# A fused state-space and MLP layer on one core: the squared halves added on VectorE before PE sums them, the x bias written by ScalarE, and four reorderings of the steady turn

## The reference

```python
x = L0_attn_x                                  # (8, 512, 128)
xn = _layernorm(x, axis=-1)
x = x + _L0_attn_ref(xn, ...) + _L0_ffn_ref(xn, ...)
```

```python
zxbcdt = x @ in_proj_w.T                       # z (256), xBC (256 + 128), dt (4)
dt = softplus(zxbcdt[..., -NHEADS:] + dt_bias)
conv = conv_b
for k in range(D_CONV):                        # 4 taps
    conv = conv + xp[:, k:k + L, :] * conv_w[:, k]
xBC = silu(conv)                               # x_ssm, B, C
theta = clip(theta_base + tanh(x @ theta_w1) @ theta_w2, ...)
log_z = complex(-lambda_eff * dt, theta * dt)  # decays and turns the state
# scan over chunks: y = Re(C . sum of exp(cumulated log_z) * B * (x_ssm * dt))
g = (y + x_ssm * D) * silu(z)
g = g * rsqrt(mean(g * g, axis=-1) + RMS_EPS) * norm_w      # 256 channels
return g @ out_proj_w.T
```

## Time and profile before

| | |
|---|---|
| time, median of 3 runs (lowest to highest) | 336.48 us (335.78 to 337.73) |
| the profiled execution: time, span of its instructions | 337.05 us, 334.9 us |
| granted TensorE clock, mean over the span | 0.964 of full |
| PE busy | 292.5 us, 87% |
| PE's weight loads | 210.1 us, 63% |
| DVE busy | 257.8 us, 77% |
| POOL busy | 190.9 us, 57% |
| ACT busy | 182.1 us, 54% |

### The profile page before, as it was taken

How to read it: one execution, slowest core, us unless ns; L and a number is a source line. 1 busy time by engine, 2 the same in 40 slices (tenths; PEclk the granted TensorE clock), 3 DMA queues, 4 the chain that set the end, 5 groups by cost and what they waited for, 6 DMA issues and landing times.

```text
span 334.9 us, 9439 instructions
## 1 busy us (share of the span) xinstructions
PE 292.5 (87%) x3927; PEld 210.1 (63%) x3927; DVE 257.8 (77%) x632; ACT 182.1 (54%) x336; POOL 190.9 (57%) x165
## 2 busy tenths in 40 slices
PE   1396679799999999999999999999899999968780
PEld 1253246587588758776678657875777577735680
DVE  4585788889788887988698878987798868887221
ACT  0587646287438844785567654774288445750110
POOL 1004253529990999279944997099918991684001
PEclk9879799999999999999999999999999999998795
DMA  7302300141012200230123001311022002301001
GB/s 204 82 0 50 78 0 2 33 97 33 31 35 68 61 18 25 77 78 2 33 57 91 16 31 41 76 45 33 3 64 66 3 31 50 81 0 34 2 2 37
DMA packets 19306, 14.85 MB, mean 44 GB/s; under 512 B 5077, under 2 KB 15034, under 8 KB 19258
## 3 DMA queue, kind: packets, MB, share of 16 engines
q1 hardware_dynamic: 17192, 13.83, 16.0%
q10 hardware_dynamic: 2066, 0.36, 0.6%
HBM read 3.70 MB, written 2.10 MB: 17 GB/s over the span
## 4 chain that ended last, share of the span: by engine, by line
PE 65%; DVE 10%; POOL 7%; ACT 6%; issue 3%; DMA 3%; SPq 2%; ACTq 1%; POOLq 0%; DVEq 0%
PE bank L1483 10%; PE bank L1534 7%; PE bank L1535 6%; PE bank L1585 4%; PE bank L1646 4%; PE bank L1545 4%; PE bank L1592 4%; PE bank L1555 4%; PE bank L1621 3%; PE bank L1636 3%; PE bank L1565 3%; ACT z L1107 2%; PE bank L1601 2%; PE bank L1523 2%; SPq L439 2%
## 5 line engine op out<-in xcount | busy, mean ns | idle before, releaser
L1332 POOL TENSOR_TENSOR btmp<-cims,X 128x512 f32<-128x512 f32 x15 | 19.1, 1272 | 68.0 <-DMA cims<-bc 53.0
L1534 PE MATMUL bank<-h0h,W 128*128 128x512 f16 x128 | 50.3, 393 | 6.9 <-DVE h1l L808 5.5
L1535 PE MATMUL bank<-h0l,W 128*128 128x512 f16 x128 | 50.0, 391 | 0.0
L1483 PE MATMUL bank<-XW,xh 128*128 128x256 f16 x256 | 48.3, 277 | 0.0
L1483 PE MATMUL bank<-XW,xl 128*128 128x256 f16 x128 | 35.3, 276 | 0.0
L1157 ACT ACTIVATE h1h<-bank 128x512 f16<-128x512 f32 x32 | 18.9, 593 | 22.7 <-PE bank L1535 22.7
L808 DVE SCALAR_TENSOR_TENSOR h1l<-bank,h1h 128x512 f16<-128x512 f32 x32 | 21.9, 687 | 11.0 <-ACT h1h L1157 10.9
L1483 PEld LDWEIGHTS bank<-XW,xh 128*128 128x128 f16 x256 | 25.3, 99 | 6.8 <-issue 0.2
L1534 PEld LDWEIGHTS bank<-h0h,W 128*128 128x128 f16 x128 | 13.9, 108 | 23.1 <-DVE h1l L808 7.0
L1113 ACT ACTIVATE tin<-bank,base 128x256 f32<-128x256 f32 x16 | 6.7, 472 | 36.5 <-PE bank L1508 36.5
L1307 POOL TENSOR_TENSOR xd<-x,dt 128x1024 f32<-128x1024 f32 x8 | 15.2, 1903 | 19.6 <-ACT x L1082 19.0
(11 more groups left out here) (196 smaller groups left out, 846.7 us busy)
## 6 DMA issues: line engine op xcount, KB each, us to landing
xtok<-in_x SPq DMA_DIRECT2D x8, 256.0 KB, 3.1
cres<-bc SPq DMA_DIRECT2D x32, 64.0 KB, 2.1
cims<-bc SPq DMA_DIRECT2D x32, 64.0 KB, 2.1
bres<-bc SPq DMA_DIRECT2D x32, 64.0 KB, 2.1
bims<-bc SPq DMA_DIRECT2D x32, 64.0 KB, 2.1
out<-osb SPq DMA_DIRECT2D x8, 256.0 KB, 2.3
const<-constants SPq DMA_DIRECT2D x1, 512.0 KB, 5.7
KT<-in_in_proj_w ACTq DMA_DIRECT2D x1, 320.0 KB, 4.5
```

What stands on the lines that cost most here:

```text
L1332: P.tensor_tensor(btmp[1][:], b[:], f2, ALU.mult).then_inc(sig.sem, 1)
L1483: last = M.matmul(dst, tok(x, c, k), w[:, k, :], start=False, stop=(k == TAPS - 1 and q == 2))
L1534: M.matmul(bank[4 + f % 2][:], w, h0h[:, k, :], start=(k == 0), stop=False)
L1535: last = M.matmul(bank[4 + f % 2][:], w, h0l[:, k, :], start=False, stop=(k == MT - 1))
```

## The change

On PE, the bias product of each x chunk goes (sequence 0 keeps one, now in 32-bit numbers from one row). Instead ScalarE writes the scaled bias into both halves of the bank before the products (`x_bias`, 128x512, two for each turn), and the products add to it. The bias is loaded as 128 equal rows instead of one; the 16-bit pair of it that DVE made at the start is gone.

In the steady turns DVE adds the two halves of gsq (`halves_added`), and PE sums one tile for each chunk (`sums_of_added`): 4 products instead of 8, in one group right ahead of `dt_products`, where before there was a group of 4 on either side of the first `mlp1` tile. DVE's `mean_squares` moves behind `decayed(n, 1)`. Turns 7 and 8 keep the old form.

Further: the transfers of cims are issued ahead of those of cres, with a semaphore for each; ScalarE computes the sine ahead of the absolute value; DVE's `states` stands behind the phases and not inside them; `h1_low(n, 2)` stands ahead of `final`; POOL's rms stands behind both halves of `b_times_rotated`.

```diff
@@ -378,7 +380,7 @@
         ]
         row_loads = [
             (tw1[:], a["theta_w1"]),
-            (cb_row[:], a["conv_b"][0:INNER].rearrange("(o c) -> o c", o=1)),
+            (conv_bias[:], row_all(a["conv_b"], INNER)),
             (s012[:, 0:1], row_all(a["s0"], 1)),
             (s012[:, 1:2], row_all(a["s1"], 1)),
             (s012[:, 2:3], row_all(a["s2"], 1)),
...
@@ -441,8 +443,8 @@
 
             def repeat_bc(n, fast):
                 sp.wait_ge(a_bc.sem, a_bc.done(n))
-                repeat_rows(STATE, cres, c_in)
-                repeat_rows(STATE + 1, cims, c_in)
+                repeat_rows(STATE + 1, cims, ci_in)
+                repeat_rows(STATE, cres, cr_in)
                 if not fast:
                     sp.wait_ge(s_bk.sem, s_bk.at(n, 0))
                 elif not (isinstance(n, int) and n == 0):
...
@@ -799,6 +802,10 @@
                         step(V.tensor_tensor(gT[:, half, cols], bank[6 + half][:, cols], z2s[p][:, half, cols], ALU.mult),
                              linked=False)
 
+            def halves_added(n):
+                v.wait_ge(a_gsq.sem, a_gsq.done(n))
+                V.tensor_tensor(gsum[:], gsq[:, 0, :], gsq[:, 1, :], ALU.add).then_inc(s_gsum, 1)
+
             def mean_squares(n):
                 v.wait_ge(t_ms.sem, t_ms.done(n))
                 V.tensor_scalar(msq[:], sums_in, EPS, None, ALU.add).then_inc(s_msq.sem, 1)
...
@@ -848,16 +855,13 @@
                     h0_low(n, 2)
                     h0_low(n, 3)
 
-                def new_states(slot):
-                    if slot == 1:
-                        states(n - 1)
-
                 if has_next:
                     early_layernorm(n + 1)
                 if has_front:
                     masks()
                     thetas(n)
-                    phases(n, new_states)
+                    phases(n)
+                    states(n - 1)
                     exponents(n, True, gates, low_tiles)
                 else:
                     masks()
...
@@ -867,11 +871,15 @@
                     xn_low(n + 1)
                 if has_front:
                     decayed(n, 0)
-                if has_back:
+                if has_back and has_next:
+                    halves_added(n - 1)
+                elif has_back:
                     mean_squares(n - 1)
                 if has_front:
                     h1_low(n, 0)
                     decayed(n, 1)
+                if has_back and has_next:
+                    mean_squares(n - 1)
                 if has_front and not has_next:
                     b_times_rotated_im(n)
                     h1_low(n, 1)
...
@@ -889,10 +897,11 @@
                     dt_input(n + 1)
                 if has_next:
                     dt_steps(n + 1)
+                if has_front:
+                    h1_low(n, 2)
                 if has_back:
                     final(n - 1, pq, stored)
                 if has_front:
-                    h1_low(n, 2)
                     h1_low(n, 3)
                     decayed(n, 2)
                 if has_next:
...
@@ -954,7 +962,6 @@
                 setup(V.scalar_tensor_tensor(low_, src, WSCALE, high, ALU.mult, ALU.subtract), False)
 
             v.wait_ge(rows_in, 16 * len(row_loads))
-            pair(CB[0:1, :], CB[BLK:BLK + 1, :], cb_row[:], BIAS_SCALE)
             for k in range(2):
                 setup(V.memset(TW1[k][:, LORA:], 0.0), False)
             pair(TW1[0][:, 0:LORA], TW1[1][:, 0:LORA], tw1[:], WSCALE)
...
@@ -1080,6 +1087,18 @@
+
+            def x_bias(n, half):
+                if not (isinstance(n, int) and n < 2):
+                    act.wait_ge(s_gate.sem, s_gate.done(n - 2))
+                step(a_bias, A.activation(bank[6 + half][:].rearrange("p (c e) -> p c e", e=INNER),
+                                          view(conv_bias, 0, 128, 0, [[0, 2], [1, INNER]]), ACT.Copy, scale=PS))
+
...
@@ -1121,8 +1141,8 @@
             def trig(n):
 
                 act.wait_ge(s_ph.sem, s_ph.at(n, PHASE_STEPS))
+                step(a_trig, A.activation(psn, phl[:], ACT.Sin, scale=TURN))
                 step(a_abs, A.activation(pabs[:], phl[:], ACT.Abs))
-                step(a_trig, A.activation(psn, phl[:], ACT.Sin, scale=TURN))
                 act.wait_ge(a_abs.sem, a_abs.done(n))
                 step(a_trig, A.activation(pcs, pabs[:], ACT.Sin, scale=-TURN, bias=halfpi[:, 0:1]))
 
...
@@ -1218,10 +1240,14 @@
                 if has_front:
                     decay_up(n)
                     mlp_high(a_h1, t_h1, h1h, n, (0,))
+                if has_next:
+                    x_bias(n + 1, 1)
+                if has_front:
                     decay_down(n)
                     mlp_high(a_h1, t_h1, h1h, n, (1,))
                     range_checked(n)
                 if has_next:
+                    x_bias(n + 1, 0)
                     dt_exp(n + 1)
                     newest_tap(n + 1)
                 if has_front:
...
@@ -1325,13 +1353,14 @@
                     P.tensor_tensor(dst[:], btmp[0][:], btmp[1][:], op).then_inc(s_cb.sem, 1)
                     g.wait_ge(s_cb.sem, s_cb.at(n, 3 * k + 3))
 
-            def turned(sig, n, re, im, left, other=None, later_factor=None, between=None):
+            def turned(sig, n, re, im, left, other=None, later=(), between=None):
 
                 (a, b), (c, d) = left
                 for k, (dst, f1, f2, op) in enumerate(((re, c, d, ALU.subtract), (im, d, c, ALU.add))[:1 if other else 2]):
                     P.tensor_tensor(btmp[1][:], b[:], f2, ALU.mult).then_inc(sig.sem, 1)
-                    if later_factor and k == 0:
-                        g.wait_ge(*later_factor)
+                    if k == 0:
+                        for awaited in later:
+                            g.wait_ge(*awaited)
                     P.tensor_tensor(btmp[0][:], a[:], f1, ALU.mult).then_inc(sig.sem, 1)
                     g.wait_ge(sig.sem, sig.at(n, 3 * k + 2))
                     if other:
...
@@ -1342,13 +1371,14 @@
                         between()
 
             def c_rotated(n, other=None):
-                g.wait_ge(c_in.sem, c_in.done(n))
+                g.wait_ge(ci_in.sem, ci_in.done(n))
                 g.wait_ge(a_trig.sem, a_trig.at(n, 1))
-                turned(s_rot, n, Rre, Rim, ((cres, cims), (pcs, psn)), other, (a_trig.sem, a_trig.done(n)))
+                turned(s_rot, n, Rre, Rim, ((cres, cims), (pcs, psn)), other,
+                       ((cr_in.sem, cr_in.done(n)), (a_trig.sem, a_trig.done(n))))
 
             def b_times_rotated(n, other=None, between=None):
                 g.wait_ge(b_in.sem, b_in.done(n))
-                turned(s_v, n, Ure, Uim, ((bres, bims), (Rre[:], Rim[:])), other, None, between)
+                turned(s_v, n, Ure, Uim, ((bres, bims), (Rre[:], Rim[:])), other, (), between)
 
             def b_and_k(n, ready, part, other=None):
 
...
@@ -1382,8 +1412,9 @@
                 if has_back and (shared or not has_front):
                     rms_of(n - 1)
                 if has_front:
-                    b_times_rotated(n, (s_im.sem, s_im.at(EDGES.index(n), 3)) if shared else None,
-                                    None if shared else lambda: rms_of(n - 1))
+                    b_times_rotated(n, (s_im.sem, s_im.at(EDGES.index(n), 3)) if shared else None)
+                    if not shared:
+                        rms_of(n - 1)
                     b_and_k(n, s_kq, 0, (s_im.sem, s_im.done(EDGES.index(n))) if shared else None)
                     if not shared:
                         b_and_k(n, s_kq, 1)
...
@@ -1471,16 +1502,18 @@
 
             def x_part(n, half, part):
 
+                first = isinstance(n, int) and n == 0
                 if part == 0:
                     pe.wait_ge(s_xl.sem, s_xl.done(n))
-                    if half == 1 and not (isinstance(n, int) and n < 2):
-                        pe.wait_ge(s_gate.sem, s_gate.at(n - 1, 0))
+                    if not first:
+                        pe.wait_ge(a_bias.sem, a_bias.at(n - 1, 2 - half))
                 c, k = 2 * half + part // TAPS, part % TAPS
                 dst = bank[6 + half][:, INNER * (c % 2):INNER * (c % 2) + INNER]
-                if k == 0:
-                    M.matmul(dst, biasrow[:], CB[:], start=True, stop=False)
+                if first and k == 0:
+                    M.matmul(dst, scale_row[:], conv_bias[0:1, :], start=True, stop=True)
                 for q, (x, w) in enumerate(pairs(XW)):
-                    last = M.matmul(dst, tok(x, c, k), w[:, k, :], start=False, stop=(k == TAPS - 1 and q == 2))
+                    last = M.matmul(dst, tok(x, c, k), w[:, k, :], start=False, stop=True,
+                                    skip_group_check=True)
                 if part == 2 * TAPS - 1:
                     last.then_inc(t_x.sem, 1)
 
...
@@ -1637,6 +1670,12 @@
                                         start=(half == 0), stop=(half == 1))
                 if c == NCH - 1:
```

(50 more changed lines are left out.)

8 lines of the change are left out of this document (4 added, 4 removed).

## The result

The changed kernel takes **358.9 us** (median; 357.72 to 362.48) against 336.74 of the kernel before beside it: ratio 1.068, interval 1.059 to 1.076. It is slower, as forecast, but outside the predicted range. Ratios here leave disturbed runs out, so they can differ a little from the quotient of two medians. The profiled execution took 358.01, with a span of 356.2 (334.9 before): 21.3 us to find.

What follows compares the result with a forecast made beforehand. Two clocks of nearly one length, PE's work and POOL's chain, were taken to bound the kernel, the wait ahead of dt deciding. 337.05 + 2.6 + 4.2 - 1.2 = 342.5, plus 5.9 for the clock: 348.5, range 340 to 352.5.

Steps and rivals of the forecast that it cites:

- The bias products, 1.17 a turn: PE, steady turns: dropping the bias products gives 0.55 ahead of the B and C products and 0.62 behind.
- The first group of sums gives nothing: PE: removing the first group (0.81) gives nearly nothing, as the MLP tile behind waits 0.6 for DVE's low half.
- K unchanged, dt 1.6 late by position, 0.7 more by POOL: Six turns: K stays; the copy behind DVE's addition, low half and Q makes dt 1.6 late; POOL adds 0.7.
- POOL's advance, -1.2: POOL's second product starts 1.23 earlier, with cres, so PE no longer waits for POOL in the long turn: -1.2.
- a fall in 4 or 5 of the six turns: PE's sparse work ahead of dt drops the clock to 1.2 GHz where x products follow, 1.3 each: +5.9.
- In the setup ... 0, give or take 0.5: DVE saves 0.7 on the bias; a 128-row transfer and four 32-bit PE products cost it back: 0, within 0.5.
- Turns 0, 7 and 8 keep their chains: The first turn and the last two were to run as before; the sum has no term for them.
- the terms ahead of the clock: Full clock: 337.05 + 2.6 (late dt less bias products) + 4.2 (addition beside POOL) - 1.2 (POOL's advance) = 342.5.
- "Slower": Whole kernel slower than the kernel before: chance 0.83, against 0.07 for the same and 0.10 for faster.
- the late dt with falling clock: The forecast's own case: the clock falls in most turns, with the late dt: 348.5, 345.5 to 352.5; chance 0.52.

Runs made afterwards that it cites:

- experiments 2, 3, 5: Changed kernel with spare PE products around the new sums: 345.0 us; with addition, sums and copy all placed earlier: 342.1 us; with the sums as before: 335.0 us.
- experiment 4: Changed kernel with the addition in VectorE's scalar form: 362.5 us, one run; with one operand of the addition in PSUM: 355.2 us, ratio 1.057.

## Why the prediction was wrong, step by step

- **The bias products, 1.17 a turn: right to the digit.** The rest of a turn went from 15.33 to 14.16 wherever the clock held and PE waited for nothing in it (experiments 2, 3, 5).
- **The first group of sums gives nothing: borne out.** In turn 2 the MLP tile behind its place starts 15.67 from the turn's start, after a wait of 0.54 for the low half (the row of 123.89 above), against 15.77 before. PE is through with the second tile 0.9 early, as forecast, and waits.
- **K unchanged, dt 1.6 late by position, 0.7 more by POOL: right.** The turns with an addition of 0.68 show 3.77 - 2.12 = 1.65; the mean is 2.16, with an addition of 1.20 where I took 1.3. The Trainium skill's page on SBUF ("SBUF — State Buffer", section "SBUF: two separate sides") says that a VectorE operation with two SBUF inputs and a GpSimd operation that reads SBUF exclude each other for a whole instruction; by that rule the PSUM operand frees both, and the traces of experiment 4 agree (0.68 and 1.27). The Trainium skill's page that I weighed in the prediction, Advanced Engine Details and Errata, gives this operation no form that blocks, and the runs decide against it.
- **POOL's advance, -1.2: right in what it gives, not in every turn's size.** From turn 2 on no product of POOL's ends a wait of PE, as one did before (240.90), and none does with the old sums either, where PE is early. But in turns 2 and 3 POOL's second product waited 0.91 and 1.90 for the DMA of cres, so the advance of 1.23 that I took for every turn, and the 1.8 for the addition of turn 3, did not come: it took 0.68 there.
- **The clock, "a fall in 4 or 5 of the six turns", "4.5 x 1.3 = +5.9": the mechanism right, the term mis-sized.** It fell in all six and cost 1.66, 1.66, 1.66, 1.67, 1.35 and 2.90 over 14.16, together 10.9. I had taken a low stretch for 2.5 us, the piece of it in turn 7 in which PE was busy; it lasts 3.4, and where dense work fills it, it costs 1.66. In turn 6 it was twice as long. In turns 5 and 6 part of it lay in PE's wait, where it cost nothing.
- **"In the setup ... 0, give or take 0.5": wrong, and the step that failed.** It was +7.4 in the profile; the two kernels that change only this put it at 4 to 5 us on the mean of their executions, the one with full rows at 7. I worked out no length for the four products, and never asked at what clock the 48 x products of that block would run. The 7.4 are three pieces. PE begins the block 0.9 later; the kernel before with one-row products, which loads the row as before, began as late (19.55), so the 128-row load isn't shown to be the cause. The block is 7.8 longer: 4 x (1.15 - 0.32) = 3.3 are the bias products themselves, 4.5 the low level under the x products. And 1.4 are given back in turn 0, where before PE made seven MLP products at 0.43 each, and after all at 0.22:

```profile
35.30 0.63 PE L1535 MATMUL bank<-h0l,W 128*128 128x512 f16 x1
35.72 0.63 PE L1534 MATMUL bank<-h0h,W 128*128 128x512 f16 x1
```

- **Turns 0, 7 and 8 keep their chains:** their work is as before, but a fall of the clock of before did not occur in turn 0 (1.4, above) nor in turn 7 (1.33 of the 1.6 gained behind the steady turns). Nothing in the prediction spoke for either: they made the miss 2.7 us smaller by luck.

The sum (the terms ahead of the clock add to 342.65, which I gave as 342.5): 348.4, +7.4 for the setup, +5.0 for the clock, -0.9 for the addition and POOL, -1.6 at the end, -0.3 outside the span: 358.0, as measured. "Slower" had 0.83 and the late dt with falling clock was the likeliest case; the range, 340 to 352.5, would have held either of the two misses, the setup or the clock, but not both.

Three things stay open. That one row, rather than the little longer time of these products (1.15 against 1.02 each), holds the clock back rests on one kernel with full rows. And when it rises with one-row products varies between executions (23.5 to behind 34); no run here shows what decides that. And the reorderings were never run apart from the bias on ScalarE.

## What to carry to other kernels

Where work is taken from a busy engine and put on another ahead of something that it must wait for, price the place before the work: four products saved cost 2.2 us a turn by standing behind DVE's queue. Then ask what the wait does to TensorE's clock: here it cost nearly as much again (1.7 to 1.8 a turn), and filling the gaps with products that nobody needs won 14 us (3 of them startup). The rest of this change (the bias on ScalarE, with the reorderings) was worth 2 to 3% once freed of the new sums and of the one-row products; six times 1.17, the bias products of PE, is 7.0 of the 7.6 us by which its six steady turns are shorter (205.9 against 213.5). So test the parts of a bundle apart.

## What the runs showed that I had not expected

- With four f32 products of one row among 48 dense 16-bit ones, the dense ones stayed at 0.21 us apiece for up to 15 us without any gap on PE; with 128 rows in the same four products the spacing fell to 0.11 at 22.2.
- The lock is symmetrical: in the changed kernel the addition ends 0.54 to 0.55 behind the POOL product under way (in five turns of six; 0.63 in the other), and POOL's next takes 1.60 to 1.73 for 1.27; one operand in PSUM ends both.
